# Graph layers on one core: run 5's third tile moved to TensorE, SyncE's start reordered, three smaller edits

## The chip, the cores and the metric

The kernel runs on one core of a Trainium2 chip. The metric is the device time of one execution in microseconds (us), lower is better. The engines of the core run their own instruction streams and meet at semaphores: TensorE (PE in the profile) multiplies, with its weight loads listed apart (PEld); VectorE (DVE) and ScalarE (ACT) do elementwise work; GpSimd (POOL) issues indirect gathers; SyncE (SP) issues the other transfers.

## The reference

Four layers of a graph network over 1250 nodes with 512 features and 40,000 edges, which come sorted by destination, then a residual and a layer norm:

```python
def _gine_layer(x, src, dst, edge_attr, eps, We, be, W1, b1, gamma, beta, W2, b2):
    e = edge_attr @ We + be
    m = relu(x[src] + e)
    agg = segment_sum(m, dst, num_segments=x.shape[0])
    h = ((1.0 + eps) * x + agg) @ W1 + b1
    h = (h - mean(h, axis=0)) * rsqrt(var(h, axis=0) + BN_EPS) * gamma + beta
    h = relu(h)
    return relu(h @ W2 + b2)
# four layers on x, src, dst, edge_weight1; then
x = layernorm(x + layers(x))
```

All of it is in float32.

## The kernel before

**Tiling.** The 40,000 edges are 313 tiles of 128, and a step takes 32 tiles: 10 steps a layer, the last with 25. A step works in 8 quads of tiles. For each tile, the rows x[src] + be of its 128 edges have to be in SBUF; VectorE then forms max(row, -w We) (`messages`, L1500), which is the message up to a term that is added per node, and TensorE multiplies the tile with a one-hot of the destinations inside a window of 32 nodes (`sum_quad`, L1889). Sums of 16 tiles are placed into blocks of 128 nodes (`open_block`, `add_first_pair`, `close_block`), and `product_h` (L2018) multiplies the block with W1, one step behind. After the last step come the rest of the block, the batch norm and the dense part `dense` (L2061), which also makes the next layer's table of rows.

**Two ways to a row.** Most tiles are gathered by GpSimd from the table in DRAM (`gather_quad`, L812), one indirect DMA a tile, into the slot of `rows` that an earlier quad leaves (it waits for `quad_summed`). The others, "near" tiles, hold edges whose sources lie in 256 nodes that are in SBUF as `table_parts`: VectorE makes a one-hot of the sources (`make_src_onehot`, L1327), TensorE multiplies it with the table (`gather_tiles`, four matmuls a tile, L1940), and ScalarE's relu (L991) gives the messages. The table is held in two parts, a rounded one that ScalarE makes (`hi_part`, L626) and the rest, which VectorE subtracts (`lo_part`, L633). Two partitions of each one-hot hold the edge's weight and two of each table part hold We; SyncE loads them (`load_w_rows`, L680, one for each near tile, and `load_We_rows`, L670). The source numbers of the near tiles are spread to 126 partitions in `src_bc` by `spread_src` (L711) from the DRAM array `near_srcs`.

**Runs.** In the first nine steps 8 tiles in a row are a run: 36 runs, four a step. At the start of the execution the edges of each run are reordered on the core so that its near tiles are full of near edges: the keys of the edges are turned on TensorE, moved in ten rounds (`move_lanes`, L1395), turned back, and laid down by `place_lanes` (L915) and L1438. Runs from 4 on with an even number have three near tiles, odd ones two, except the runs in `EXTRA_RUNS` (9, 13, ... 33), which have a third. In the first four runs there is one more near tile, tile 5. A layer so has 99 near tiles of 313, three tiles of the last step are loaded by SyncE row by row (`load_rows`, L694), and GpSimd gathers 211. These 7 + 4 extra tiles are collected apart: `make_extra_onehot` (L905, L909) on ScalarE makes a one-hot of 7 x 128 for each, and `sum_extra` (L1815) on TensorE sums with it; nine before the lanes are placed, two after. The results go through `finish_near` (L1459 to L1473) on VectorE to `near_srcs` and `near_ws`. A count on the core checks that each run holds as many near edges as its tiles take (128 each); where one doesn't, the flag sends all engines into a slow path that handles one tile at a time.

**Order of the work around the change.** Each engine's order is written out by hand. SyncE at the start: inputs; the ten blocks of the table as they are staged (L1407, written at L655), W1 (L664), then, when ScalarE has made `near_src` (L925), that array to DRAM (L716), its spread, the We rows, the weights of the near tiles to DRAM (L721), their rows, the extra tiles. GpSimd in each layer: 12 early gathers (`gather_early`), then `layer_begins`, which waits until the whole table is written and x is updated, a wait on `lo_ready` until all table parts are subtracted, and the other gathers in order. In the first layer also the sums of the edge weights are made: ScalarE copies them (`copy_w`), `place_w` (L1873, L1877) places them on TensorE behind quad 1, VectorE reduces them (`keep_w`, L1385) and adds them times We to u (`finish_u`). In the last step `keep_w` stands behind the messages of quad 2, ahead of those of quad 3.

## Time and profile before

| | before |
|---|---|
| median of 3 runs | 1306.46 us (1304.39 to 1312.17) |
| profiled execution, time | 1306.36 us |
| profiled execution, span | 1304.6 us |
| PE busy (share of the span) | 1196.9 us (92%) |
| DVE busy | 1030.8 us (79%) |
| POOL busy | 806.2 us (62%) |
| ACT busy | 527.2 us (40%) |
| mean granted TensorE clock | 0.949 of full |
| gathers on GpSimd | 844, 211 a layer |
| matmuls of `gather_tiles` | 1584, 4 for each of 99 tiles a layer |

The span goes from the first to the last instruction of the profiled execution. Busy shares are means over stages with different limits: the start (to some 96 us), four layers with ten steps each, and a dense part after each layer. In the rows below a line of a timeline gives the start, the duration, the engine and line, the operation with its operands, and in brackets how long the engine was idle before and what ended that. SPq is SyncE's queue issuing a DMA; the duration is the issuing alone. In the chain of waits a DMA's duration reaches to its landing.

### The profile page before, as it was taken

What the parts mean: (1) busy time and instruction counts of PE and PEld (TensorE: products, weight loads), DVE (VectorE), ACT (ScalarE), POOL (GpSimd) and SP (SyncE); (2) the same over time, 40 slices, a digit from 0 to 9 for tenths busy, and PEclk for the clock granted to TensorE, in tenths of its full rate; (3) what the DMA queues carried; (4) which work ended last, traced back from release to release, by engine and by line L of the source; (5) the groups of instructions that cost most, each with busy time, mean ns of one, the idle gap of its engine ahead of it and who ended that gap; (6) DMA issues with size and microseconds to landing.
All of it is one profiled execution on the core that took longest, in us unless ns stands there. A gap on an engine that the chain in (4) does not pass through costs nothing.

```text
span 1304.6 us, 24990 instructions
## 1 busy us (share of the span) xinstructions
PE 1196.9 (92%) x7338; PEld 750.9 (58%) x7338; DVE 1030.8 (79%) x2120; ACT 527.2 (40%) x1155; POOL 806.2 (62%) x855
## 2 busy tenths in 40 slices
PE   3838999999898999999798999999798999999797
PEld 2834666666544666566454566656455566665453
DVE  7968889888768878887767978787766978778677
ACT  1833343434274343334174334333254434334233
POOL 0047777777317777777607777777705777777720
PEclk7559999999899999999899999999798999999899
DMA  3158777777547777777737777777746777777753
GB/s 112 55 185 254 215 215 215 216 214 215 170 134 225 216 215 214 216 215 215 241 104 229 214 216 214 215 215 215 235 128 204 215 214 216 215 215 215 225 177 110
DMA packets 93131, 259.25 MB, mean 199 GB/s; under 512 B 19527, under 2 KB 22780, under 8 KB 92992
## 3 DMA queue, kind: packets, MB, share of 16 engines
q0 software_dynamic: 67520, 221.30, 58.2%
q1 hardware_dynamic: 25472, 36.29, 8.5%
q8 instruction: 63, 1.03, 0.3%
q14 instruction: 76, 0.62, 0.1%
HBM read 244.36 MB, written 12.96 MB: 197 GB/s over the span
## 4 chain that ended last, share of the span: by engine, by line
POOL 42%; PE 32%; issue 14%; DVE 8%; DMA 3%; SPq 0%; POOLq 0%; ACT 0%; DVEq 0%
POOL rows L812 42%; PE y_ps L2061 9%; PE y_ps L1940 7%; PE pair_ps L1889 6%; PE h_ps L2018 3%; DVE rows L1500 2%; DVE rows L1395 2%; PE y_ps L2072 1%; PE uT_ps L1971 1%; DMA rows<-node_table,src_fast 1%; PE uT_ps L1978 1%; PE uT_ps L1964 1%; DMA node_table<-rows 1%; PE pair_ps L2004 1%; DVE rows L1407 1%
## 5 line engine op out<-in xcount | busy, mean ns | idle before, releaser
L812 POOL DMA_INDIRECT rows<-node_table,src_fast x844 | 803.5, 952 | 444.2 <-issue 256.7
L1500 DVE SCALAR_TENSOR_TENSOR rows<-We_ps,negw_fast,rows 128x512 f32<-128x512 f32 x844 | 581.9, 743 | 155.3 <-DMA rows<-node_table,src_fast 154.6
L991 ACT ACTIVATE rows<-y_ps 128x512 f32<-128x512 f32 x396 | 234.2, 603 | 497.4 <-PE y_ps L1940 493.7
L1940 PE MATMUL y_ps<-table_parts,src_onehot 128*128 128x512 f32 x1584 | 419.1, 412 | 15.3 <-DVE table_parts L633 8.0
L1940 PEld LDWEIGHTS y_ps<-table_parts,src_onehot 128*128 128x128 f32 x1584 | 281.3, 190 | 208.3 <-issue 99.4
L1889 PE MATMUL pair_ps<-rows,onehot 128*32 128x512 f32 x2504 | 323.8, 615 | 38.8 <-DVE rows L1500 38.5
L1889 PEld LDWEIGHTS pair_ps<-rows,onehot 128*32 128x32 f32 x2504 | 62.0, 109 | 174.2 <-issue 105.5
L1327 DVE TENSOR_TENSOR src_onehot<-y_ps,src_bc 126x256 fp32r<-126x256 f32 x356 | 138.9, 412 | 3.0 <-PE y_ps L1940 3.0
L2018 PEld LDWEIGHTS h_ps<-uT,W_sb 128*128 128x128 f32 x1152 | 134.3, 192 | 7.0 <-issue 4.2
L2018 PE MATMUL h_ps<-uT,W_sb 128*128 128x128 f32 x1152 | 135.2, 276 | 0.0
L2061 PE MATMUL y_ps<-rows,hT 128*128 128x512 f32 x288 | 124.5, 593 | 0.0
L2061 PEld LDWEIGHTS y_ps<-rows,hT 128*128 128x128 f32 x288 | 54.4, 190 | 67.9 <-issue 59.8
L1091 ACT ACTIVATE hT<-hT,bn_bias,bn_scale 128x128 f32<-128x128 f32 x160 | 65.5, 480 | 6.6 <-DVE bn_bias L1546 6.6
L1004 ACT ACTIVATE hT<-h_ps,vec 128x128 f32<-128x128 f32 x144 | 41.2, 370 | 59.0 <-PE h_ps L2018 59.0
L978 ACT COPY pair_sb<-pair_ps 128x512 f32<-128x512 f32 x76 | 44.3, 583 | 42.0 <-PE pair_ps L1889 42.0
L1692 DVE TENSOR_TENSOR rows<-y_ps,b_bc 128x512 f32<-128x512 f32 x36 | 24.8, 688 | 37.4 <-PE y_ps L2061 37.4
L1315 DVE TENSOR_TENSOR onehot<-y_ps,local_all 128x512 f32<-128x512 f32 x80 | 53.5, 669 | 0.6 <-DVE w_sum L1385 0.3
L1971 PE MATMUL uT_ps<-place,pair_sb 128*128 128x96 f32 x304 | 46.0, 297 | 0.0
L1971 PEld LDWEIGHTS uT_ps<-place,pair_sb 128*128 128x128 f32 x304 | 40.5, 207 | 3.4 <-issue 3.4
L1978 PEld LDWEIGHTS uT_ps<-place,pair_sb 128*128 128x128 f32 x288 | 37.0, 201 | 6.7 <-issue 6.7
L1815 PE MATMUL h_ps<-hT 128*128 128x2 f32 x154 | 32.3, 344 | 8.3 <-ACT hT L909 8.3
L1978 PE MATMUL uT_ps<-place,pair_sb 128*128 128x64 f32 x288 | 39.4, 282 | 0.0
(248 smaller groups left out, 779.0 us busy)
## 6 DMA issues: line engine op xcount, KB each, us to landing
late_rows<-node_table SPq DMA_DIRECT2D x1536, 2.0 KB
rows<-node_table,src_fast POOLq DMA_INDIRECT x844, 3.7
node_table<-rows SPq DMA_DIRECT2D x29, 256.0 KB, 3.4
src_onehot<-near_ws SPq DMA_DIRECT2D x396, 2.0 KB
x_now<-x_pad SPq DMA_DIRECT2D x10, 512.0 KB, 7.6
W_sb<-W SPq DMA_DIRECT2D x4, 1024.0 KB, 5.3
rows<-W SPq DMA_DIRECT2D x16, 256.0 KB, 4.0
out<-rows SPq DMA_DIRECT2D x8, 256.0 KB
```

Of the source, the lines that this page charges most:

```text
L812: nc.gpsimd.indirect_dma_start(rows[:, slot, :], None, table[:, :], bass.IndirectOffsetOnAxis(src_fast[:, t:t + 1], 0)).then_inc(landed[q] ...
L991: nc.scalar.activation(rows[:, slot, :], y_ps[k % 2][:, :], ACT.Relu).then_inc(tile_ready, 1)
L1091: nc.scalar.activation(hT[:, c, at:at + P], hT[:, c, at:at + P], ACT.Relu, bias=bn_bias[:, c:c + 1], scale=bn_scale[:, c:c + 1]).then_inc( ...
L1315: return nc.vector.tensor_tensor(to, cols_ps[:, 0:WIN].unsqueeze(1).to_broadcast([P, tiles, WIN]), local_all[:, at:at + tiles].unsqueeze(2 ...
L1327: nc.vector.tensor_tensor(src_onehot[0:USED, at:at + 2, :], nodes[0:USED, :].unsqueeze(2).to_broadcast([USED, 2, P]), src_bc[0:USED, sprea ...
L1500: last = nc.vector.scalar_tensor_tensor(rows[:, slot, :], We_ps[:, :], negw_fast[:, t:t + 1], row, ALU.mult, ALU.max)
L1889: last = nc.tensor.matmul(pair_ps[h][WIN * win:WIN * (win + 1), :], onehot[:, h, tile - h * PAIR, :], rows[:, slot, :], start=t in firsts, ...
L1940: last = nc.tensor.matmul(y_ps[k % 2][:, :], src_onehot[:, 2 * (k % ONEHOTS) + b, :], table_parts[:, part, 2 * pair_of(k) + b, :], start=( ...
L1971: nc.tensor.matmul(sums_of(c, l, i)[:, 0:PLACED], pair_sb[:, 0, f], place0(i), start=False, stop=False, skip_group_check=True)
L1978: last = nc.tensor.matmul(uT_ps[:, c, HALF:P], pair_sb[:, 1, c * P:(c + 1) * P], place1(i, 0, HALF), start=False, stop=True, skip_group_ch ...
L2018: last = nc.tensor.matmul(h_ps[:, c, :], W1_sb[:, k, c * P:(c + 1) * P], uT[:, k, :], start=(k == 0), stop=(k == C - 1))
L2061: last = nc.tensor.matmul(y_ps[m % 3][:, :], hT[:, c, at:at + P], W2_sb[:, c, :], start=(c == 0), stop=(c == C - 1))
```

## The change

One more run, number 5, gets a third near tile: `EXTRA_RUNS` begins at run 5, `TWO_RUNS` becomes a single slice, `EXTRA_TILES` goes from 11 to 12 and the near tiles of a layer from 99 to 100, the gathers from 211 to 210. Nine extra one-hots stay on ScalarE; the last three (two before) are made by VectorE with a comparison, behind the subtraction of the We rows' parts and ahead of the scaling of the row numbers, and ScalarE's two are dropped. Two small arrays move into slots of `rows` that are free at that time. GpSimd no longer waits for `lo_ready` after `layer_begins`. In the first layer's last step `place_w` stands behind quad 0 instead of quad 1. SyncE writes seven blocks, then sends `near_src` to DRAM, then writes the last three blocks, sends the near weights, spreads the sources, loads the first weight rows, and only then the We rows and W1.

```diff
--- before.py
+++ after.py
@@ -103,13 +103,13 @@
     KINDS = 3
     FIRST_RUNS, LATER_RUNS = slice(0, LONG_A_STEP), slice(LONG_A_STEP, LONG_RUNS)
     THREE_RUNS = slice(LONG_A_STEP, LONG_RUNS, 2)
-    EXTRA_RUNS = slice(2 * LONG_A_STEP + 1, LONG_RUNS, LONG_A_STEP)
-    TWO_RUNS = [slice(LONG_A_STEP + 1, LONG_A_STEP + 2), slice(LONG_A_STEP + 3, LONG_RUNS, LONG_A_STEP)]
+    EXTRA_RUNS = slice(LONG_A_STEP + 1, LONG_RUNS, LONG_A_STEP)
+    TWO_RUNS = slice(LONG_A_STEP + 3, LONG_RUNS, LONG_A_STEP)
     THIRDS = (LONG_RUNS - LONG_A_STEP) // 2
     EXTRAS = list(range(LONG_RUNS)[EXTRA_RUNS])
     FIRST_EXTRA = LONG - 3
     EXTRA_TILES = len(EXTRAS) + LONG_A_STEP
-    EXTRAS_BEFORE = EXTRA_TILES - 2
+    EXTRAS_BEFORE = EXTRA_TILES - 3
     SOON_STAGED = 7
     LATER_EXTRAS, FIRST_EXTRAS = slice(0, len(EXTRAS)), slice(len(EXTRAS), EXTRA_TILES)
     EARLY_BELOW = 3 * P - MARGIN + 34
@@ -310,10 +310,10 @@
         extra_edges = hT[:, 0, GUARD + 2 * P:GUARD + 2 * P + 2 * LONG * EXTRA_TILES].rearrange("p (e j v) -> p e j v", j=LONG, v=2)
         minus_place = sb("minus_place", [P, EXTRA_TILES, LONG])
         near_first = sb("near_first", [P, LONG_A_STEP, LONG], bf16)
-        chosen_first = sb("chosen_first", [P, LONG_A_STEP, LONG])
+        chosen_first = spare(15, LONG_A_STEP * LONG, SORTED_TILES).rearrange("p (r j) -> p r j", j=LONG)
         minus_from = sb("minus_from", [P, 1])
         run_delta = sb("run_delta", [P, LONG_RUNS])
-        within = sb("within", [P, SORTED_TILES], i32)
+        within = spare(13, SORTED_TILES).bitcast(i32)
         node_in = sb("node_in", [P, 2])
 
 
@@ -597,10 +597,8 @@
                     (THREE_RUNS, slice(7, 8), last[:, rest_lanes(THREE_RUNS), 0:1]),
                     (EXTRA_RUNS, slice(3, 7), first[:, rest_lanes(EXTRA_RUNS), :]),
                     (EXTRA_RUNS, slice(7, 8), last[:, rest_lanes(EXTRA_RUNS), 0:1]),
-                    (TWO_RUNS[0], slice(2, 6), first[:, rest_lanes(TWO_RUNS[0]), :]),
-                    (TWO_RUNS[0], slice(6, 8), last[:, rest_lanes(TWO_RUNS[0]), :]),
-                    (TWO_RUNS[1], slice(2, 6), first[:, rest_lanes(TWO_RUNS[1]), :]),
-                    (TWO_RUNS[1], slice(6, 8), last[:, rest_lanes(TWO_RUNS[1]), :]),
+                    (TWO_RUNS, slice(2, 6), first[:, rest_lanes(TWO_RUNS), :]),
+                    (TWO_RUNS, slice(6, 8), last[:, rest_lanes(TWO_RUNS), :]),
                     (FIRST_RUNS, slice(2, 5), first[:, early_lanes, 0:3]),
                     (FIRST_RUNS, slice(6, 8), first[:, rest_lanes(FIRST_RUNS), 0:2])]
 
@@ -701,10 +699,11 @@
                 for c in range(C):
                     sp.dma_start(row_numbers(m)[:, c, :], src_t[ROW_PIECE * c:ROW_PIECE * (c + 1), t:t + 1].rearrange("p o -> o p"),
                                  allow_slow_non_contiguous=True).then_inc(row_numbers_loaded, 16)
-            for k in range(BLOCKS):
-                sp.wait_ge(staged, k + 1)
-                write_block(k)
-            load_W1(0)
+            def write_blocks(a, z):
+                for k in range(a, z):
+                    sp.wait_ge(staged, k + 1)
+                    write_block(k)
+
             def spread_src(g):
                 for a, z in SPREAD[g]:
                     at = SPREAD_AT[a]
@@ -712,16 +711,19 @@
                                  near_srcs[a:z, :].rearrange("(o b) p -> o (b p)", o=1).to_broadcast(
                                      [USED, (z - a) * P])).then_inc(src_spread[g], 16)
 
+            write_blocks(0, SOON_STAGED)
             sp.wait_ge(sort_act, NEAR_SRC_READY)
             sp.dma_start(near_srcs[0:P, :], near_src[:, :]).then_inc(near_src_written, 16)
+            write_blocks(SOON_STAGED, BLOCKS)
+            sp.wait_ge(sort_dve, NEAR_W_READY)
+            sp.dma_start(near_ws[0:P, :, :], near_w[:, :, :].bitcast(fp32)).then_inc(near_w_written, 16)
             sp.wait_ge(near_src_written, 16)
             spread_src(0)
-            load_We_rows(0)
-            sp.wait_ge(sort_dve, NEAR_W_READY)
-            sp.dma_start(near_ws[0:P, :, :], near_w[:, :, :].bitcast(fp32)).then_inc(near_w_written, 16)
             sp.wait_ge(near_w_written, 16)
             for k in range(EXTRA_AT):
                 load_w_rows(0, k)
+            load_We_rows(0)
+            load_W1(0)
             sp.wait_ge(extra_src_ready, 1)
             sp.dma_start(near_srcs[P:P + EXTRA_TILES, :], extra_src[0:EXTRA_TILES, :]).then_inc(near_src_written, 16)
             sp.wait_ge(extra_w_ready, 1)
@@ -845,7 +847,6 @@
                 for l in range(L):
                     gather_early(l)
                     layer_begins(l)
-                    pool.wait_ge(lo_ready, PARTS_A_LAYER * (l + 1))
                     for q in range(QUADS):
                         gather_quad(q, 0, False)
                     for i in range(1, BLOCKS):
@@ -928,9 +929,7 @@
             nc.scalar.copy(lane_values[:, 1, :], lane_ints[:, 1, :]).then_inc(sort_act, 1)
             nc.scalar.mul(near_w[:, 0, :], lanes[:, 1, 0:P].bitcast(fp32), -0.5).then_inc(sort_act, 1)
             place_lanes(src_fast, turned_src, SRC_TURNED)
-            make_extra_onehot(EXTRAS_BEFORE)
             place_lanes(negw_fast, turned_w, LAST_TURNED)
-            make_extra_onehot(EXTRAS_BEFORE + 1)
             for k in range(WRITTEN[0], BLOCKS):
                 act.wait_ge(staged, k + 1)
                 hi_part(k)
@@ -1423,6 +1422,14 @@
                                            near_w[:, 0, :], ALU.mult, ALU.subtract).then_inc(sort_dve, 1)
             dve.wait_ge(We_hi_ready, 1)
             nc.vector.tensor_tensor(We_lo[0:1, :], We_bc[0:1, :], We_hi[0:1, :], ALU.subtract).then_inc(We_parts_ready, 1)
+            then_wait(nc.vector.tensor_scalar(minus_place[:, EXTRAS_BEFORE:EXTRA_TILES, :], minus_place[:, EXTRAS_BEFORE:EXTRA_TILES, :],
+                                              -1.0, None, ALU.mult))
+            for e in range(EXTRAS_BEFORE, EXTRA_TILES):
+                dve.wait_ge(extra_summed, e - 2)
+                nc.vector.tensor_tensor(
+                    extra_onehot(e), cols[:, 0:P].unsqueeze(1).to_broadcast([P, LONG - 1, P]),
+                    minus_place[:, e, 0:LONG - 1].unsqueeze(2).to_broadcast([P, LONG - 1, P]),
+                    ALU.is_equal).then_inc(extra_onehot_ready, 1)
             dve.wait_ge(row_numbers_loaded, 16 * C * len(ROW_TILES))
             places = hT[0:len(ROW_TILES), :, ROW_GUARD:ROW_GUARD + ROW_PIECE].bitcast(i32)
             nc.vector.tensor_scalar(places, places, float(ROW_BYTES), None, ALU.mult).then_inc(row_places_ready, 1)
@@ -1900,6 +1907,8 @@
                         pe.wait_ge(pair_copied[q // 4], n + 1)
                         pe.wait_ge(onehot_ready, 2 * n + q // 4 + 1)
                     sum_quad(q, l, i)
+                    if q == 0 and l == 0 and final:
+                        place_w(i)
                     if final:
                         gather_tiles(l, QUADS * i + q)
                     elif q % 2:
@@ -1915,7 +1924,7 @@
                             product_h(n - 1, l, i - 1)
                     if q == 0 and l == 0 and i == 0:
                         sum_w(0)
-                    if q == 1 and l == 0:
+                    if q == 1 and l == 0 and not final:
                         place_w(i)
                     if q == 3 and final:
                         open_block(n, l, i, True)
```

## Rows read from the trace of the kernel before

**Rows 1.** The page: chain that ended last; costliest group (busy, mean ns | idle before).

```profile
POOL 42%; PE 32%; issue 14%; DVE 8%; DMA 3%; SPq 0%; POOLq 0%; ACT 0%; DVEq 0%
...
L812 POOL DMA_INDIRECT rows<-node_table,src_fast x844 | 803.5, 952 | 444.2 <-issue 256.7
```

**Rows 2.** Chain of waits, 60 to 135 us: start us, us, what.

```profile
74.34 5.50 DMA near_srcs<-near_src
...
80.22 5.01 DMA src_bc<-near_srcs
...
95.83 5.57 PE y_ps L1940 x16
```

**Rows 3.** Timeline of the start, in order of time: start us, us, engine line op.

```profile
71.33 0.40 ACT L925 ACTIVATE near_src<-rows,minus_from 128x128 uint8<-128x128 int32 x1
...
73.83 0.47 SPq L664 DMA_DIRECT2D W_sb<-W  x1
...
75.53 0.23 DVE L1438 COPY local_all<-pair_ps 128x64 f32<-128x64 f32 x1 [1.18 <-PE y_ps L1826]
...
76.80 0.52 DVE L1445 TENSOR_TENSOR local_all<-local_all,run_delta 128x128 f32<-128x128 f32 x4
...
80.75 3.06 PEld L1815 LDWEIGHTS h_ps<-hT 128*128 128x128 f32 x14 [2.13 <-ACT hT L909]
...
93.41 0.95 POOL L812 DMA_INDIRECT rows<-node_table,src_fast  x1 [3.64 <-DVE table_parts L633]
```

**Rows 4.** Landing of the W1 load; then DMA issues (median us to landing last).

```profile
DMA to landing us min/median/max: 5.8/5.8/5.8
...
rows<-node_table,src_fast POOLq DMA_INDIRECT x844, 3.7
...
eps_cur<-eps SPq DMA_DIRECT2D x4, 0.5 KB, 2.6
```

**Rows 5.** Timeline: a copy of 864 elements at the start; a gather before the second layer.

```profile
26.96 0.93 DVE L1309 COPY rows<-rows 128x864 f32<-128x864 f32 x1
...
395.52 1.36 POOL L812 DMA_INDIRECT rows<-node_table,src_fast  x1 [0.30 <-issue]
```

**Rows 6.** First layer, steps 0 and 1: timeline of SyncE and TensorE.

```profile
118.45 0.25 SPq L680 DMA_DIRECT2D src_onehot<-near_ws  x1
...
120.73 0.25 SPq L680 DMA_DIRECT2D src_onehot<-near_ws  x1
...
122.46 1.06 PE L1889 MATMUL pair_ps<-rows,onehot 128*32 128x512 f32 x8 [1.30 <-DVE rows L1500]
...
129.00 2.14 PE L1940 MATMUL y_ps<-table_parts,src_onehot 128*128 128x512 f32 x8
```

**Rows 7.** First layer's last step: timeline, then a window (counts, PEclk, DMA share, GB/s).

```profile
332.38 1.94 PE L1889 MATMUL pair_ps<-rows,onehot 128*32 128x512 f32 x8 [2.26 <-DVE rows L1500]
...
341.81 0.94 POOL L812 DMA_INDIRECT rows<-node_table,src_fast  x1 [0.30 <-issue]
...
342.66 0.16 DVE L1385 TENSOR_REDUCE w_sum<-h_ps 128x1 f32<-128x3 f32 x1 [5.16 <-PE h_ps L1877]
...
351.77 1.91 PE L1889 MATMUL pair_ps<-rows,onehot 128*32 128x512 f32 x12
...
330.00:342.00 12.00, 9.74 (x49) 6.15 (x46) 7.50 (x12) 1.64 (x5) 8.95 (x11) 0.57 0.80 255
```

**Rows 8.** Start of the second layer: timeline.

```profile
396.30 0.69 DVE L633 TENSOR_TENSOR table_parts<-rows,table_parts 126x512 fp32r<-126x512 f32 x1 [0.24 <-ACT table_parts L626]
...
400.08 1.09 ACT L991 ACTIVATE rows<-y_ps 128x512 f32<-128x512 f32 x2 [3.71 <-DMA node_table<-rows]
```

**Rows 9.** Third layer: timeline of TensorE, two of the products h; the waits of layer 4.

```profile
736.92 3.74 PE L2018 MATMUL h_ps<-uT,W_sb 128*128 128x128 f32 x32
...
812.89 3.74 PE L2018 MATMUL h_ps<-uT,W_sb 128*128 128x128 f32 x32
...
PE pair_ps L1889 <- DVE rows L1500: 9.4, 10, 3.1
```

## The prediction

> **What bounds the kernel now.** The profiled execution took 1306.36 us for a span of 1304.6 us. It stands 0.10 us from the median of the three runs shown (1306.46), so a difference against it is one against the median. I read the page first: the chain that ended last runs for 42% of the span through GpSimd's gathers and for 32% through TensorE [rows 1]. A gather costs 0.952 us and 0.30 us of issue behind it, 1.254 us in all, 844 times. Then the chain in order of time. It has two parts. From the start to about 360 us, where layer 1 of 4 ends, no gather is in it: it is the start (VectorE, SyncE's small transfers, VectorE again) and then TensorE. In layers 2 to 4 it follows the gathers one by one, about 250 us a layer, with the dense part between.
>
> The start has one place that waits for transfers. ScalarE has the near source numbers ready at 71.33 + 0.40 = 71.73 us [rows 3]. SyncE sends them at 74.34 only, behind the last block's write and the W1 load; they land 5.50 us later, at 79.84, and their spread to 126 partitions lands at 85.23 [rows 2]. Only then can VectorE make the first source one-hots. TensorE's first gather by matmul starts at 95.83 [rows 2].
>
> **SyncE's order.** The numbers' write now stands in front of blocks 7 to 9 and of W1. What does it take there? Ahead of it was W1, issued at 73.83 and landed after 5.8 us, at 79.6, just before the write at 79.84 [rows 3, 4]. A small transfer without such company takes 2.6 us [rows 4]. So it goes at 71.8 and lands between 74.4 (2.6) and 77.3 (5.5 again). I take 74.4, since the W1 load is what stood ahead of it. The Trainium skill (DMA: Bandwidth & Descriptors, Queues, rings and completion order) says that a DMA engine consumes one ring's descriptors in ring order; by that rule the write is free of W1 and 74.4 is right, without it the engines were merely loaded and 77.3 is.
>
> The spread takes 85.23 - 79.84 = 5.4 us again, landing at 79.8 to 82.7. Three block writes are in flight beside it, so I take 80.6: **4.6 us earlier**, with ends at 2.5 and, from VectorE's side, 5.8 us, as follows.
>
> **VectorE's new work.** The one-hots of the last three extra tiles come from ScalarE to VectorE, before the copies of rows that start at 75.53 after an idle 1.18 us and end at 76.80 + 0.52 = 77.32 [rows 3]. The trace has no comparison of 896 elements; the nearest row is a copy of 864, 0.93 us [rows 5]. I take 1.0 each, 0.9 to 1.1, and 0.2 for the sign: 3.2 us. VectorE is through at 77.32 - 1.18 + 3.2 = 79.3, before the spread at 80.6. The work is covered by that wait, with 1.3 us to spare; if the spread came earlier, 79.4 would be the floor. TensorE's three sums of 14 weight loads at 3.06 us (the slower kind, [rows 3]) end by 75.5 + 9.2 = 84.7. VectorE asks for them after its five subtractions, which ended near 92.6 and will near 88: covered.
>
> Two-input work on VectorE touches GpSimd too: a gather beside the subtractions of table parts, one of them at 396.30, took 1.36 instead of 0.95 us [rows 5, 8]. The new one-hots run beside the first early gathers: three times 0.4, 1.2 us. I count nothing, since GpSimd has slack in this layer (below). The Trainium skill (SBUF — State Buffer, Who interferes with whom) has a harder rule against this change: a VectorE instruction with two SBUF inputs keeps a GpSimd instruction that reads SBUF off the shared port for its whole length. By it the early gathers would lose up to 3.2 us; the row shows less.
>
> **The rest of SyncE's queue.** Moved back are the We rows (four DMAs) and W1. The weights' write goes at 74.0 and lands 2.6 to 5.8 us later; four weight rows and four We rows at up to 0.47 each follow, so the We rows are issued by 80.4 to 83.6 and land by 89.4 at the latest. TensorE needs them at 95.83 - 4.6 = 91.2. W1, issued by 84.1, is first read in step 1, past 130. The extra tiles' write comes at about 89.7, when W1 (by 89.9) has just landed: 0 to 0.2 us.
>
> **GpSimd's dropped wait.** In layer 1 it held the gathers back 3.64 us, to 93.41 [rows 3]. With one gather less GpSimd would be 4.9 us ahead. But it is not the bound there: its last gather is issued at 341.81 and lands 3.7 us later at 345.5 [rows 4, 7], while the last matmuls of the step stand at 351.77 [rows 7], some 6 us later. TensorE's side moves by 4.6 us, so the slack stays. The wait would also have ended with VectorE's subtractions, at 88.0. Worth 0. In later layers the last subtraction is done at 396.99, the table's write only at 400.08 [rows 8], which GpSimd waits for anyway. Worth 0.
>
> **The third tile of run 5.** Per layer it removes one gather and one VectorE message, and adds four matmuls, one source one-hot (VectorE), one relu (ScalarE) and one weight row (SyncE). Two such tiles take TensorE 2.14 us, so 1.07 each [rows 6]. Layer 1: the tile's matmuls fall in step 0, just before 122.46, where TensorE waits 1.30 us for VectorE [rows 6]. They fit. VectorE gives up a message for a shorter one-hot. Worth 0, at worst 1.1 us. Layers 2 to 4: one gather less on the path, 1.254 us each, **3.8 us**. That holds if TensorE has room. Its own pace is (812.89 - 736.92) / 3 = 25.3 us a step [rows 9]; 21 gathers take 26.3. It starts behind and catches up, and then waits for VectorE's rows, 9.4 us in layer 4 [rows 9]. The change asks 1.25 + 1.07 = 2.3 of those. Enough is left.
>
> **Weights placed behind quad 0 in the last step of layer 1.** VectorE waited 5.16 us for them [rows 7]. That goes. What is late next? TensorE itself: after 332.38 it never waits for VectorE to the end of the step (its last group ran from 351.77 without an idle, [rows 7]), and the moved matmuls are the same. The cover is TensorE's own queue. Worth 0.
>
> **Sum.** 4.6 + 3.8 = 8.4 us: 1306.36 - 8.4 = **1298.0 us**, 0.6% less. Ends: 2.5 + 3.8 - 1.1 = 5.2 gives 1301.2; 5.8 + 3.8 = 9.6 gives 1296.8; with the spread of runs, 1295.5 to 1302.
>
> **Rivals.**
> 1. The start does not move: the spread lands near 85 again since the DMA engines, not W1, are the limit. Then 3.8 remain: 1302.6. For it: three writes and the gathers run at that time. Against: the landing just behind W1. 0.09.
> 2. TensorE is the bound in layers 2 to 4: 3 x 1.07 more instead of 3.8 less, 1306.36 - 4.6 + 3.2 = 1305.0. Against: 9.4 us of waiting. 0.03.
> 3. Slower: SyncE's rows. For each near tile it sends a weight row and four late rows, one round in 120.73 - 118.45 = 2.28 us [rows 6], against 25.3 / 11 = 2.30 us a tile on TensorE. If this queue decided, each extra tile would cost 2.28 us in four layers, 9.1: 1306.36 - 4.6 + 9.1 = 1310.9. It decides where a row's issue less than some 3 us precedes its tile. The tiles at 129.00 used the row issued at 118.45 and the one after; with one tile more they use that of 120.73 first, 8.3 us ahead. 0.02.
> 4. The clock. Before the last step of layer 1 TensorE waits 2.26 us, and the next eight matmuls take 1.94 us where eight take 1.06 elsewhere [rows 6, 7]; the granted clock was 0.57 of full from 330 to 342 us, mostly the 1.2 GHz level [rows 7]. Over the 10 us from 332.4 on that costs about 10 x (1 - 1.06 / 1.94) = 4.5 us where TensorE is the path. If shifted waits spare one: 1293.5. 0.07.
> 5. The change doesn't do what it says: run 5 must hold 128 edges with sources among 252 nodes in seven tiles, else the slow path runs, far above all this. Expected are 896 x 252 / 1250 = 181. 0.01.
>
> The likeliest case has 0.78.
>
> **Range and chances.** A measurement tells 1% (13 us) from no change. Only case 4 comes to 1293.3, half of it, and a little of the likeliest: faster 0.07. Slower by over 1%: case 5 and some of 3: 0.02. The rest, 0.91, is within 1%. The range of 8 in 10 takes in the likeliest, case 1 and the edge of case 4: 1294 to 1303.
>
> **What would show it.** The numbers' write in about 2.6 us, the spread landed before 82; TensorE's first gather by matmul near 91; VectorE's one-hots about 1 us each and no wait behind them; 840 gathers; VectorE's wait of 5.16 us gone and the layer's end moved only as much as its start; layers 2 to 4 each 1.25 us shorter from the first to the last gather. I am wrong if the spread again lands 5 us after its issue behind something else, or if TensorE's waits for rows vanish in layer 4.

## The result and the profile after

The changed kernel takes 1300.35 us (median of 6 runs, 1296.56 to 1301.59), the kernel before beside it 1308.94 (6 runs, 1304.39 to 1312.17): ratio 0.9929, 95% interval [0.9911, 0.9947]. A second comparison gave 1300.31 against 1308.98 (e9, below). So it is 8.6 us less, where the forecast's sum was 8.4, and 1300.35 lies in the forecast's range of 1294 to 1303. The likeliest value, 1298.0, is 2.35 us lower, mainly since the forecast set out from 1306.36 and the median of the kernel before is 1308.94 over six runs. The profiled execution took 1299.8 us, 6.56 less than that of before.

The page of the changed kernel: chain that ended last, then the group of the gathers, which answer to [rows 1].

```profile
POOL 39%; PE 36%; issue 14%; DVE 8%; DMA 2%; ACT 0%; DVEq 0%
...
L814 POOL DMA_INDIRECT rows<-node_table,src_fast x840 | 800.3, 953 | 439.8 <-issue 256.5
```

840 gathers instead of 844; the chain is the same kind. The lines of before stand some lines lower (a gather at L814, a VectorE message at L1507, a quad's sum at L1896, a gather by matmul at L1949).

Timeline of the start of the changed kernel, SyncE, VectorE, GpSimd and TensorE, answering to [rows 2, 3]:

```profile
71.50 0.33 SPq L716 DMA_DIRECT2D near_srcs<-near_src  x1
72.00 1.53 SPq L653 DMA_DIRECT2D node_table<-rows  x3
73.58 0.45 SPq L719 DMA_DIRECT2D near_ws<-near_w  x1
74.08 0.90 SPq L710 DMA_DIRECT2D src_bc<-near_srcs  x2
...
80.01 0.45 SPq L662 DMA_DIRECT2D W_sb<-W  x1
...
74.09 3.10 DVE L1429 TENSOR_TENSOR hT<-cols,minus_place 128x896 f32<-128x896 f32 x3
...
78.48 0.52 DVE L1452 TENSOR_TENSOR local_all<-local_all,run_delta 128x128 f32<-128x128 f32 x4
80.39 1.43 DVE L1326 TENSOR_TENSOR src_onehot<-node_in,src_bc 126x256 fp32r<-126x256 f32 x4 [1.40 <-issue]
...
74.50 1.65 POOL L814 DMA_INDIRECT rows<-node_table,src_fast  x1 [71.19 <-ACT src_fast L916]
76.46 1.55 POOL L814 DMA_INDIRECT rows<-node_table,src_fast  x1 [0.30 <-issue]
...
91.08 6.73 PE L1949 MATMUL y_ps<-table_parts,src_onehot 128*128 128x512 f32 x16 [2.13 <-issue]
```

The write of the source numbers goes at 71.50. It lands in 16 parts in the trace, the last at 72.90: it takes 1.4 us, not 5.5. SyncE sends the spread, which waits for it, only at 74.08, since three block writes and the near weights stand between in its queue. The last landing of the spread in the trace is at 78.35 (85.23 in the kernel before; both traces hold 30 of its 32 landings). VectorE's first source one-hot comes 1.40 us after its last copy, at 80.39. The chain of waits shows what its queue does in that time: L1599 loads the flag of the slow path, L1763 branches on it.

```profile
79.22 0.55 DVEq L1599
79.80 0.21 DVEq L1599
80.11 0.06 DVEq L1763
```

TensorE's first gather by matmul moves from 95.83 to 91.08, **4.75 us** (4.6 forecast). VectorE's three one-hots take 3.10 us.

Where the rest went is read at TensorE's first matmuls of each layer's dense part (the part behind the last step). I call the time between two of these a layer. Before: 360.12, 661.01, 961.80, 1262.46. After: 354.88, 655.21, 955.60, 1255.90. Layer 1's end came 5.24 us earlier, but layers 2 to 4 gave only 0.56, 0.40 and 0.36 in this profile, 1.3 in sum, where 3.8 were forecast. The last step of layer 2 shows why: TensorE's timeline of the changed kernel, then a window (counts, PEclk, DMA share, GB/s).

```profile
625.64 1.94 PE L1896 MATMUL pair_ps<-rows,onehot 128*32 128x512 f32 x8 [3.70 <-DVE rows L1507]
...
635.68 1.94 PE L1896 MATMUL pair_ps<-rows,onehot 128*32 128x512 f32 x8
637.55 4.94 PE L2027 MATMUL h_ps<-uT,W_sb 128*128 128x128 f32 x32
642.41 1.06 PE L1896 MATMUL pair_ps<-rows,onehot 128*32 128x512 f32 x8
```

```profile
619.00:640.00 21.00, 16.29 (x72) 9.31 (x73) 15.17 (x24) 2.41 (x4) 15.94 (x17) 0.51 0.78 246
```

Eight matmuls of 512 columns take 1.94 us here and 1.06 behind it: TensorE was granted the level of 1.2 GHz for some 20 us, after waits for VectorE's rows. From quad 0's sum, at 625.64, to the dense part took 29.57 us; in the kernel before 28.18, with a low stretch of some 10 us:

```profile
629.00:649.00 20.00, 16.18 (x100) 10.84 (x100) 13.92 (x22) 2.44 (x5) 15.12 (x17) 0.74 0.82 261
```

So layer 2 reached its last step 1.9 us sooner and gave 1.4 back there; in the mean of layers 2 to 4 it is 1.5 and 1.1. Whether it does so each time is what experiment e9 had to settle.

In layer 1's last step the order of the placed weights is changed as the diff says. The changed kernel, TensorE, then VectorE, answering to [rows 7]:

```profile
328.18 1.07 PE L1896 MATMUL pair_ps<-rows,onehot 128*32 128x512 f32 x8 [2.25 <-DVE rows L1507]
329.17 0.53 PE L1880 MATMUL h_ps<-pair_w,place 128*128 128x3 f32 x2
...
333.22 0.14 DVE L1384 TENSOR_REDUCE w_sum<-h_ps 128x1 f32<-128x3 f32 x1
...
350.13 0.42 DVE L1595 COPY uT<-y_ps 128x256 f32<-128x256 f32 x1 [3.63 <-PE y_ps L1998]
```

VectorE's 5.16 us of waiting are gone, and it waits 3.63 us for TensorE later: TensorE was the cover, as forecast. GpSimd issued its last gather of the layer at 338.37 (341.81 before), 3.4 us earlier, not the 4.9 of the forecast.

### The profile page after: what moved, and what is told of

The parts are those of the page before. It is cut to its first block, busy times and chain, and to the rows that moved or that the text cites. A ratio compares the mean times of both kernels' runs of the same rounds, so it can differ in the third digit from the quotient of the medians.

```text
span 1298.0 us, 25044 instructions
## 1 busy us (share of the span) xinstructions
PE 1205.2 (93%) x7367; PEld 759.7 (59%) x7367; DVE 1032.9 (80%) x2122; ACT 523.0 (40%) x1139; POOL 803.0 (62%) x851
## 4 chain that ended last, share of the span: by engine, by line
POOL 39%; PE 36%; issue 14%; DVE 8%; DMA 2%; ACT 0%; DVEq 0%
POOL rows L814 39%; PE y_ps L2070 10%; PE y_ps L1949 7%; PE pair_ps L1896 7%; PE h_ps L2027 3%; DVE rows L1507 2%; DVE rows L1394 2%; PE uT_ps L1980 1%; PE y_ps L2081 1%; PE uT_ps L1987 1%; PE uT_ps L1973 1%; DMA rows<-node_table,src_fast 1%; PE uT_ps L1962 1%; DMA node_table<-rows 1%; PE pair_ps L2013 1%
## 5 line engine op out<-in xcount | busy, mean ns | idle before, releaser
L814 POOL DMA_INDIRECT rows<-node_table,src_fast x840 | 800.3, 953 | 439.8 <-issue 256.5
L1507 DVE SCALAR_TENSOR_TENSOR rows<-We_ps,negw_fast,rows 128x512 f32<-128x512 f32 x840 | 579.2, 742 | 156.8 <-DMA rows<-node_table,src_fast 156.1
L1949 PE MATMUL y_ps<-table_parts,src_onehot 128*128 128x512 f32 x1600 | 420.9, 409 | 13.9 <-DVE table_parts L631 8.0
L1949 PEld LDWEIGHTS y_ps<-table_parts,src_onehot 128*128 128x128 f32 x1600 | 282.5, 189 | 207.8 <-issue 94.8
L1896 PE MATMUL pair_ps<-rows,onehot 128*32 128x512 f32 x2504 | 322.2, 616 | 33.9 <-DVE rows L1507 33.4
L1896 PEld LDWEIGHTS pair_ps<-rows,onehot 128*32 128x32 f32 x2504 | 62.2, 109 | 167.2 <-issue 103.1
L2027 PEld LDWEIGHTS h_ps<-uT,W_sb 128*128 128x128 f32 x1152 | 137.2, 196 | 8.5 <-issue 5.8
L2027 PE MATMUL h_ps<-uT,W_sb 128*128 128x128 f32 x1152 | 138.1, 279 | 0.0
L1822 PE MATMUL h_ps<-hT 128*128 128x2 f32 x168 | 36.5, 353 | 4.8 <-ACT hT L910 4.8
```

Of the source, the lines that this page charges most:

```text
L814: nc.gpsimd.indirect_dma_start(rows[:, slot, :], None, table[:, :], bass.IndirectOffsetOnAxis(src_fast[:, t:t + 1], 0)).then_inc(landed[q] ...
L1507: last = nc.vector.scalar_tensor_tensor(rows[:, slot, :], We_ps[:, :], negw_fast[:, t:t + 1], row, ALU.mult, ALU.max)
L1896: last = nc.tensor.matmul(pair_ps[h][WIN * win:WIN * (win + 1), :], onehot[:, h, tile - h * PAIR, :], rows[:, slot, :], start=t in firsts, ...
L1949: last = nc.tensor.matmul(y_ps[k % 2][:, :], src_onehot[:, 2 * (k % ONEHOTS) + b, :], table_parts[:, part, 2 * pair_of(k) + b, :], start=( ...
L2027: last = nc.tensor.matmul(h_ps[:, c, :], W1_sb[:, k, c * P:(c + 1) * P], uT[:, k, :], start=(k == 0), stop=(k == C - 1))
```

## Experiments

All times below are medians, and the ratios are to the kernel before, run beside them on the same chip. Experiments e1 to e4 shared one comparison, e5 to e8 another, e9 to e12 a third; only the third has the changed kernel in it. Where a dense part is dated, it is TensorE's first matmul there in the profiled execution.

**e1, SyncE's old order** (the other three parts kept).

```
-            write_blocks(0, SOON_STAGED)
+            write_blocks(0, BLOCKS)
+            load_W1(0)
             sp.wait_ge(sort_act, NEAR_SRC_READY)
             sp.dma_start(near_srcs[0:P, :], near_src[:, :]).then_inc(near_src_written, 16)
...
```

> The changed kernel with SyncE's order at the start as it was (W1 and all ten blocks ahead of the source numbers). Theory A (the start's gain is SyncE's order alone): the numbers' write again takes about 5.5 us, the spread lands near 85, TensorE's first gather by matmul starts at 95 to 96 instead of 91.08 us, the dense part of layer 1 begins about 4.7 us later than 354.88, the whole near 1304.5 us against 1299.8 for the changed kernel's profiled execution. Rival B (the start was won by taking one-hots off ScalarE or by the dropped wait): first gather by matmul stays near 91 and the time near 1300.

1302.2 us (4 runs), ratio 0.9944 [0.9926, 0.9963]. SyncE's and VectorE's timeline of e1:

```profile
74.07 0.55 SPq L717 DMA_DIRECT2D near_srcs<-near_src  x1
80.00 0.77 SPq L710 DMA_DIRECT2D src_bc<-near_srcs  x2
...
85.55 1.43 DVE L1325 TENSOR_TENSOR src_onehot<-node_in,src_bc 126x256 fp32r<-126x256 f32 x4 [6.56 <-DMA src_bc<-near_srcs]
```

The write takes 5.9 us again and the first gather by matmul starts at 96.29, as theory A had it. The whole gain of the start is SyncE's order. Layer 1's dense part began at 362.76, 7.9 us later than in the changed kernel and not 4.7: its last step had a longer stretch at the low clock (table below).

**e2, without the third tile of run 5.**

```
-    EXTRA_RUNS = slice(LONG_A_STEP + 1, LONG_RUNS, LONG_A_STEP)
-    TWO_RUNS = slice(LONG_A_STEP + 3, LONG_RUNS, LONG_A_STEP)
+    EXTRA_RUNS = slice(2 * LONG_A_STEP + 1, LONG_RUNS, LONG_A_STEP)
+    TWO_RUNS = [slice(LONG_A_STEP + 1, LONG_A_STEP + 2), slice(LONG_A_STEP + 3, LONG_RUNS, LONG_A_STEP)]
...
```

> The changed kernel without run 5's third tile (99 near tiles and 211 gathers a layer; VectorE still makes three extra one-hots). Theory A (in layers 2 to 4 the time from one dense part to the next is set by the low clock in the last step, which swallowed most of the tile's gain): these distances, 300.33, 300.39 and 300.30 us with the tile, become 300.7 to 300.9 without it, so the whole is 1.3 us slower. Rival B (the tile is worth its gather, 1.25 us a layer, and something else in the change cost 0.8 a layer): they become 301.6, the whole 3.8 us slower.

1302.93 us (6 runs), ratio 0.9961 [0.994, 0.9982]; 844 gathers. Its dense parts start at 358.45, 659.37, 959.75 and 1261.66: layers of 300.92, 300.38 and 301.91 us. From a dense part to quad 0 of the next last step it takes 272.03, 271.49, 271.77 us, against 270.77 in the mean with the tile. From the 13th gather of a layer (the first behind the early ones) to its last it takes 247.6 us here in each of layers 2 to 4, against 246.3 to 246.6 in all profiles with the tile: one gather, 1.25 us. (In the kernel before it is 248.2: in that profile each gather took 3 ns more than in e2.) The layers fit neither theory by themselves, since their last steps differ by more than the theories do.

**e3, a busy TensorE ahead of the last steps.** 16 products without a use stand in the queue ahead of quad 0 of each layer's last step, so that its wait is filled.

```
+                if final:
+                    idle_products(y_ps[0][:, :], KEEP)
                 for q in range(QUADS):
```

> The changed kernel with 16 products that nobody reads on TensorE ahead of quad 0 of the last step of each layer, about 4 us, where it waits 2.3 us in layer 1 and 3.6 to 4.2 us in layers 2 to 4 for the messages. Theory A (the idle wait lowers the clock, and the low clock then sets the tail): the last step's eight matmuls take 1.06 instead of 1.94 us, product h 3.8 instead of 4.9, and each layer from 2 on is about 1.3 us shorter, until the last gather (12.2 us ahead of the dense part in the kernel before) sets the end; layer 1 gains 2 to 4 us: 1292 to 1295 in all. Rival B (the landing of the last gathers sets the end anyway): the clock is up but the distances between the dense parts stay at 300.3 us and the time at 1298 to 1300; if the products only delay quad 0, 1300 to 1302.

1295.69 us (4 runs), ratio 0.9908 [0.9888, 0.9929]. In layer 1's last step the clock was 1.00 throughout. In layers 2 to 4 quad 0's wait shrank to 1 us and its sum ran at full clock, but the low level came at a later wait; TensorE's timeline of e3, layer 4:

```profile
1222.43 1.06 PE L1897 MATMUL pair_ps<-rows,onehot 128*32 128x512 f32 x8 [1.01 <-DVE rows L1508]
...
1230.45 1.94 PE L1897 MATMUL pair_ps<-rows,onehot 128*32 128x512 f32 x8 [2.29 <-DVE rows L1508]
1232.31 5.79 PE L2030 MATMUL h_ps<-uT,W_sb 128*128 128x128 f32 x32
```

From quad 0 to the dense part it still took 28.59, 29.44 and 28.39 us. Layer 1's dense part came at 353.07, 1.8 us earlier, and the time lies between the two theories.

**e4, two one-hots of extra tiles on VectorE instead of three.**

```
-    EXTRAS_BEFORE = EXTRA_TILES - 3
+    EXTRAS_BEFORE = EXTRA_TILES - 2
```

> The changed kernel with one of VectorE's three extra one-hots made by ScalarE, which idles 8.03 us before the lanes are placed. Theory A (VectorE, not the spread of the source numbers, now sets the start: its last copy ends at 79.00, and the 1.40 us before its first source one-hot at 80.39 are the branch): everything from there on is 1.0 us earlier, first gather by matmul at 90.0, whole near 1298.8. Rival B (the spread's landing sets 80.39): the first source one-hot stays at 80.39 and the time at 1299.8.

1296.75 us (4 runs), ratio 0.9912 [0.9893, 0.9931]. The chain of waits of e4, then VectorE's timeline:

```profile
74.25 1.40 SPq L710
...
75.70 4.24 DMA src_bc<-near_srcs
```

```profile
80.05 1.45 DVE L1326 TENSOR_TENSOR src_onehot<-node_in,src_bc 126x256 fp32r<-126x256 f32 x4 [1.83 <-DMA src_bc<-near_srcs]
```

The first source one-hot comes at 80.05 instead of 80.39, the first gather by matmul at 90.73. One us less of VectorE's work gained only 0.35, since here the spread sets the start, landing at 79.93. In the changed kernel it had landed by 78.4: there VectorE was the later of the two, by about 2 us. The spread is 1.6 us later in e4 since SyncE took 1.40 us to issue its first half (0.44 in the changed kernel). The same is seen in e11 and e12, the other two kernels with two one-hots on VectorE (1.3 and 1.2 us); the cause stays open. The profiled execution's gain over that of the changed kernel, 4.4 us, came almost whole in the last steps of layers 2 to 4, in code that is the same: there the low stretches were shorter, and layer 1's dense part moved by only 0.1 us.

**e5, W1 ahead of the numbers' write**, the rest of SyncE's order as changed.

```
             sp.wait_ge(sort_act, NEAR_SRC_READY)
+            load_W1(0)
             sp.dma_start(near_srcs[0:P, :], near_src[:, :]).then_inc(near_src_written, 16)
...
             load_We_rows(0)
-            load_W1(0)
```

> The W1 load stands ahead of the near source numbers' write again, the rest of SyncE's order is that of the changed kernel. Theory A (the write took 5.5 us before because the W1 load was in front of it): W1 is issued near 71.5 us, the write some 0.5 us later and it lands only with W1, 5 to 6 us after its issue, near 77.5; the spread lands near 83 and TensorE's first gather by matmul starts near 94 instead of 91.1; time about 3 us above the changed kernel's, near 1303. Theory B (the write took long since the DMA engines were loaded at that time by the gathers and block writes, not because of W1): it lands 2.6 us after its issue as in the changed kernel, the first gather by matmul at 91.1 to 91.6, the time the same.

1302.41 us (10 runs), ratio 0.9949 [0.9933, 0.9965]. The chain of waits of e5:

```profile
71.60 0.39 SPq L662
...
72.03 6.41 DMA near_srcs<-near_src
...
78.84 5.48 DMA src_bc<-near_srcs
```

Theory A: the same write, 0.5 us later, takes 6.4 us behind the W1 load and 1.4 us ahead of it, and the first gather by matmul goes to 95.11. Theory B, that gathers and block writes were the cause, falls. The trace holds 16 landings for W1, at 77.12 to 78.28, and 16 for the write, at 77.31 to 78.44: it lands part by part just behind the load. Three block writes issued right behind the write in the changed kernel did it no harm.

**e6, weights placed behind quad 1 again in the last step.**

```
-                    if q == 0 and l == 0 and final:
-                        place_w(i)
...
-                    if q == 1 and l == 0 and not final:
+                    if q == 1 and l == 0:
```

> In layer 1's last step the weights are placed behind quad 1 again. Prediction's step (worth 0, TensorE's own queue is the cover): VectorE's wait of about 5 us for the placed weights comes back, and the time from quad 0 of that step to layer 1's dense part is within 0.5 us of the changed kernel's, apart from the clock. Rival (VectorE's wait delayed something): layer 1's dense part starts 2 us or more later than at 354.9.

1294.85 us (4 runs), ratio 0.9906 [0.9879, 0.9933]: if anything faster than with the step. TensorE's, then VectorE's timeline of e6:

```profile
327.96 1.07 PE L1896 MATMUL pair_ps<-rows,onehot 128*32 128x512 f32 x8 [2.26 <-DVE rows L1507]
...
333.24 0.34 PE L1880 MATMUL h_ps<-pair_w,place 128*128 128x3 f32 x2
...
333.98 0.16 DVE L1384 TENSOR_REDUCE w_sum<-h_ps 128x1 f32<-128x3 f32 x1 [0.89 <-PE h_ps L1884]
```

VectorE's wait is back, but with 0.89 us, not 5.16. Neither theory had that: the wait of before was long since TensorE ran that step at the low level. The wait is 0.89 us with no low stretch (e6), 2.51 with 3.4 us of one (e10) and 5.16 with 10.2 us (before). Layer 1's dense part started at 351.43, 3.45 us earlier than in the changed kernel, behind a quad 0 that differs by 0.22 us. The windows of that step, changed kernel, then e6:

```profile
328.00:338.00 10.00, 9.82 (x58) 6.67 (x58) 9.96 (x18) 1.30 (x3) 7.56 (x9) 0.66 0.81 256
```

```profile
328.00:338.00 10.00, 10.00 (x86) 7.34 (x87) 9.07 (x16) 1.83 (x3) 7.56 (x9) 1.00 0.90 293
```

**e7, GpSimd's wait for the table's split put back.**

```
                     layer_begins(l)
+                    pool.wait_ge(lo_ready, PARTS_A_LAYER * (l + 1))
```

> GpSimd waits for the split of the table again ahead of a layer's first gather. Prediction's step (worth 0): GpSimd starts its main gathers of layer 1 at the end of VectorE's subtractions, within 0.5 us of 88, and layer 1's dense part starts within 0.5 us of 354.9; in layers 2 to 4 nothing moves. Rival (without the wait GpSimd starts layers earlier): the first gathers of layer 1 come 1 us or more later than without the wait, and the time rises by as much.

1298.12 us (9 runs, 1294.23 to 1304.08), ratio 0.9935 [0.9917, 0.9952]. GpSimd's timeline of e7:

```profile
90.00 0.95 POOL L814 DMA_INDIRECT rows<-node_table,src_fast  x1 [0.30 <-issue]
91.25 0.95 POOL L814 DMA_INDIRECT rows<-node_table,src_fast  x1 [0.30 <-issue]
```

The gather at 90.00 is the last of the 12 early ones, that at 91.25 the first behind the wait. It is not held: with the start 4.7 us earlier the subtractions end at 87.57, before GpSimd gets to this wait at 90.95. The wait is worth 0, as forecast, but the gathers do not start at the subtractions' end near 88, as expected; the early ones end later than that. Layer 1's dense part began at 353.93, 0.95 us earlier than in the changed kernel.

**e8, weights placed right behind the quad's sum in every step** (quad 1, in the last step quad 0), ahead of the gathers by matmul.

```
-                    if q == 0 and l == 0 and final:
+                    if q == (0 if final else 1) and l == 0:
                         place_w(i)
...
-                    if q == 1 and l == 0 and not final:
-                        place_w(i)
```

> The weights of a block are placed on TensorE right behind the sum of quad 1 in every step of layer 1 (quad 0 in the last), ahead of the gathers by matmul that follow that sum. Theory A (the 2.26 us that TensorE waits for VectorE before layer 1's last step, and the stretch at the 1.2 GHz level behind it, come from VectorE's wait of 3.9 us for the placed weights in the step before): VectorE's wait falls under 1 us, TensorE's wait of 2.26 us shrinks under 1 us, the granted clock stays high in that step, and layer 1's dense part starts 3 to 6 us earlier than 354.9; layers 2 to 4 unchanged; time 1294 to 1298. Theory B (TensorE's wait comes from VectorE's own amount of work): VectorE's wait goes, but TensorE's stays about 2 us and the dense part moves by less than 1 us.

1295.95 us (4 runs), ratio 0.991 [0.9884, 0.9935]. Theory A holds for layer 1: clock 1.00 in its last step, dense part at 350.02, 4.86 us earlier. TensorE is no longer what this layer waits for. The chain of waits of e8, from the last but one gather of layer 1:

```profile
335.58 0.95 POOL rows L814
336.83 3.59 DMA rows<-node_table,src_fast
...
350.02 10.38 PE y_ps L2068 x24
```

The gathers now set the end of layer 1: once TensorE gains 4.9 us, nothing is left of the slack that the forecast put at some 6 us.

**e9, the changed kernel again**, unaltered, with more rounds.

> The changed kernel unaltered, run again with more rounds beside the kernel before, so that its time and its layers do not rest on one profiled execution. Theory A (the four parts are worth what the prediction's sum says, 8.4 us, and the first profile of the changed kernel only caught long stretches at the 1.2 GHz level): its layers 2 to 4 take about 299.1 us each in the profile, not 300.3, and the median stands 8 to 10 us below the kernel before. Theory B (the tail of the last step eats 1.1 us of each layer's gain every time): layers of 300.3 again and a median 6 to 7 us below.

1300.31 us (6 runs, 1295.97 to 1301.43), ratio 0.9928 [0.9909, 0.9948], 8.67 us below the kernel before (1308.98, 11 runs). Its layers took 300.44, 299.59 and 299.15 us, between the two theories (the median is in theory A's range): the first of the three had again a low stretch of 20 us and 29.59 us from quad 0 to the dense part, the others 28.93 and 28.12.

**e10, weights behind quad 1 again, a second time** (the edit of e6).

> The kernel with the weights placed behind quad 1 again in layer 1's last step, a second time, beside the changed kernel. Theory A (the place of these matmuls decides nothing; the profile of the first such run had the full clock in that step by chance): over 5 rounds its median is within 1.5 us of the changed kernel's of the same call. Theory B (behind quad 0 they bring on the stretch at the 1.2 GHz level in layer 1's last step, which then costs 3 us): the granted clock in that step is 1.00 again, the time from quad 0 to the dense part 23.5 us against 25.0, and the median is 2 to 4 us below the changed kernel's.

1296.75 us (5 runs), ratio 0.991 [0.9891, 0.9928]: 3.6 us below e9, as theory B had it, but the clock fell here too, for about 3 us. Below the two are taken apart.

**e11, combination**: e3's 16 products, e4's two one-hots, e8's place.

> Weights placed right behind the sum of quad 1 (quad 0 in the last step), 16 products without a use ahead of quad 0 in every layer's last step, and two instead of three one-hots of extra tiles made by VectorE. Theory A (the gains add as far as the chain lets them; GpSimd's gathers bound layer 1 now): dense part of layer 1 starts at 349.5 to 350.5, layers 2 to 4 take 298.4 to 299.2 each, time 1291 to 1295. Theory B (the clock takes back what one place gains): layers of 299.5 to 300.5, time as the changed kernel's within 2 us.

**1294.43 us** (5 runs, 1291.61 to 1294.8), ratio 0.9887 [0.9869, 0.9905]. That beats the kernel before by 14.6 us and the changed one, in the same comparison, by 5.9. Dense parts at 350.70, 650.90, 949.49, 1248.77; the layers took 300.20, 298.59 and 299.28 us. Time and layer 1 came nearly as theory A had them (350.70 against 349.5 to 350.5), the layers only in part: one of three lies within its 298.4 to 299.2. Several single edits stand within 2.3 us of the combination (e3, e4, e6, e8, e10) and their intervals overlap with its own, so that it beats each of them is not shown.

**e12, combination with 8 more products ahead of quad 2** of the last step.

```
                 for q in range(QUADS):
+                    if q == 2 and final:
+                        idle_products(y_ps[0][:, :], KEEP_2)
```

> As the combination, with 8 more products without a use ahead of quad 2 in each last step. Theory A (the low stretch, which came at the later wait of 2.3 us once quad 0's was filled, goes when that wait is filled too): the granted clock is 1.00 through the last 28 us of layers 2 to 4, the time from quad 0 to the dense part is 25 to 27 us instead of 28 to 29.5, layers 2 to 4 take 297 to 298, time 1287 to 1291. Theory B (TensorE waits for rows, and a higher clock there only makes it wait longer): the clock is 1.00, but the layers take 298.5 or more and the time is that of the combination within 1 us.

1293.85 us (5 runs, 1291.56 to 1296.29), ratio 0.9893 [0.9875, 0.991], as e11. The window of layer 4's last step in e12, then TensorE's timeline near its end:

```profile
1218.00:1248.00 30.00, 27.25 (x192) 18.40 (x190) 23.15 (x51) 5.31 (x15) 14.80 (x16) 1.00 0.63 206
```

```profile
1238.66 1.06 PE L1898 MATMUL pair_ps<-rows,onehot 128*32 128x512 f32 x6 [0.63 <-DVE rows L1509]
1240.26 1.70 PE L1898 MATMUL pair_ps<-rows,onehot 128*32 128x512 f32 x6 [0.54 <-DVE rows L1509]
```

Theory B: the full clock in all four last steps, yet 28.03, 28.23 and 27.71 us from quad 0 to the dense part, and layers of 299.53, 298.89 and 298.28. TensorE now waits for the last rows; the gathers are the floor of layers 2 to 4. From a layer's last gather to the dense part it takes 11.9 to 12.2 us here, and 11.8 to 14.2 in the other profiles.

## Why the prediction held, step by step

**The start: 4.6 forecast, 4.75 measured.** The mechanism is right: e1 and e5 show that the W1 load alone made the write slow (1.4 us without it in front, 5.9 and 6.4 behind it). The Trainium skill's rule of ring order (DMA: Bandwidth & Descriptors, Queues, rings and completion order) agrees with that. That the two sums are so close is in part luck, since sizes inside the step were off and nearly cancelled:

- The write took 1.4 us, not 2.6, but SyncE came to the spread only at 74.08, near the forecast's 74.4.
- The spread then took 4.3 us, not 5.4 and more, and had landed by 78.4, not 80.6.
- VectorE was through with its copies at 79.0 (79.3 forecast), but ready only at 80.39, since the forecast left out the 1.40 us of loading the flag and branching. "Covered, with 1.3 us to spare" was wrong: VectorE was the later, by about 2 us.

So the start is now set by VectorE and not, as the forecast had it, by the spread; by the forecast's own floor for that case the gain would have been 5.8 us.

**SyncE's later rows.** W1 was issued at 80.01, well inside the 84.1 allowed, and the extra tiles' write went at 89.59 (89.7 forecast). The rival of SyncE's rows (1310.9) fell with the time.

**VectorE's one-hots.** 3.10 us against 3.2. Two early gathers beside them took 1.65 and 1.55 us; at the same place in the kernel before 1.11 and 0.95, so 1.1 us lost, forecast 1.2. The Trainium skill's harder rule (SBUF — State Buffer, Who interferes with whom), read as a block for as long as VectorE works on the three, would have cost up to 3.1 us here; the rows show a third of that. Each of the two gathers lost less (0.54 and 0.60 us) than one of these instructions lasts (1.09 and 1.08), so a block by a single instruction is not ruled out. Two more early gathers were slowed, which the forecast did not count: one beside the source one-hots took 1.16 us and one beside the subtractions 1.41. So GpSimd's gathers behind the early ones began at 91.50, and GpSimd gained 3.4 us in layer 1 where the forecast had 4.9; its slack shrank, but it was enough.

**The dropped wait: 0.** Right (e7).

**The third tile: 3.8.** In the first profile it was 1.3, and this was the term that looked mis-sized. Over all profiles it was not. The 27 layers of the nine kernels that have the tile, and no added products, run from a dense part to quad 0 of the next last step in 270.68 us in the mean (270.32 to 271.55), the six of before and e2 in 272.02 (271.49 to 272.71): **1.34 us a layer**, for the 1.254 of one gather and its issue. The part behind took 28.51 with it (27.62 to 29.91) and 28.91 without (28.18 to 30.14), whole layers 299.19 and 300.93. So 1.3 us are taken away before the last step and nothing is given back on average; the changed kernel's first profile drew three of the longest last steps, 29.53 to 29.62. By the ratios, the tile is worth 0.0032 to 0.0033 of 1309 us, 4.2 to 4.3 (e2 against the changed kernel, whose intervals overlap). The rival that TensorE becomes the bound (1305.0) fell: in layer 4 TensorE still waits 9.4 us for VectorE's rows, as much as before. The forecast's 2.3 us that the tile would take out of these waits are not seen.

In layer 1 the tile cost nothing that can be seen: first gather by matmul to quad 0 of the last step 237.10 us with it, 239.53 without (e2), 236.55 before. But over e1, e3 to e7, e9 and e10, which have the tile, it scatters from 236.1 to 238.3, so a cost of up to 1.1 us, the forecast's worst case, is not ruled out.

**The placed weights: 0.** At an equal clock this is right. What decides the last step of layer 1 is how long TensorE is at the low level; whether the place of these matmuls has a part in that stays open (below). From quad 0's sum to the dense part, beside the time at the low level in that step (summed from the granted clock of windows of 1 us):

```
kernel    placed behind   at 1.2 GHz, us   quad 0 to dense part, us
e6        quad 1           0               23.47
e10       quad 1           3.4             25.09
after     quad 0           6.8             26.70
e7        quad 0           6.8             26.67
e4        quad 0           6.8             26.70
before    quad 1          10.2             27.74
e9        quad 0          10.2             27.76
e2        quad 0          10.2             27.85
e5        quad 0          10.2             27.80
e1        quad 0          13.7             29.83
```

At the same low time the two places differ by 0.1 us (before against e9, e2 and e5), and each us at the low level costs 0.4 to 0.5 us. e3 and e11, with added products and quad 0, had no low stretch and took 23.60, again 0.1 from e6. Two kernels without a low stretch took longer: e8 with 25.17 us, where the gathers set the end, and e12 with 25.51, with 8 more products in the step. This is rival 4 as a mechanism: that a low stretch is spared was priced at 4.5 us and is worth up to 4.3 (27.74 - 23.47). In the changed kernel's profile it came to 1.0. With it the 5.24 us of layer 1's end add up: 4.75 from the start and 1.04 from here, less 0.55 that lay between the first gather by matmul and that quad 0 (237.10 us against 236.55).

**What stays open.** e6 and e10 together have a median of 1295.5 us over 9 runs, the changed kernel 1300.3 over 12. In the profiles of the table the low stretches behind quad 1 were 0, 3.4 and 10.2 us long, behind quad 0 never under 6.8. It may be that the thin matmuls of the placed weights (128x3) just behind the waits of 1.26 and 2.25 us keep the clock low longer; in e1, e2, e5 and e9, though, the clock fell before they ran, and e4 and e7, with the change's place, had 1296.75 and 1298.12. The changed kernel, e4 and e7 together have 1298.15 over 25 runs, still 2.6 us above e6 and e10. Three profiles on one side do not settle it: this part of the change may be worth 0, or may cost some 3 to 5 us. For the same reason the medians of single undone parts do not add up: e1 stands 1.9 us above the changed kernel and e5 2.1, where the positions in the trace show 5.2 and 4.0 at the start. Medians of kernels that differ from the changed one only by parts forecast at 0 go from 1294.85 to 1298.12, against 1300.3 for itself. So it is luck too that the whole came out within 0.2 us of the sum; what is shown is the gain at the start and the gather less in each layer.

In layers 2 to 4 a low stretch costs less, since the gathers cover it: with 6.8 us of it, 27.77 to 28.51 us from quad 0 on, with none 27.7 to 28.2 (e12), and stretches of 17 us and over gave 28.97 to 29.62. When one comes matters too: a total of 10.2 us, part of it in the last 10 us before the dense part, gave 29.91 (e10, layer 3).

## What to carry to other kernels

Put the small transfer that others wait for ahead of the large load in its queue; whether the load is what delays it shows in one look, when it lands just behind the load. Read a transfer's time from its landing, not from when the queue sends what waits for it: the queue may be busy with other things until then. Count the loading of a flag and the branch on it (1.40 us here) on an engine's path when you judge what is "covered" by a wait of about 1 us. And do not read a change of a few us from one profile: take each layer at fixed marks, over all kernels that share its code, and read the granted clock of the last step beside it.

## What the runs showed of the hardware

A write of 16 KB (128x128 uint8) behind a load of 1 MB in the same queue took 5.5 to 6.4 us (before, e1, e5), with its landings just behind those of the load; ahead of it, and ahead of three writes of 256 KB, 1.4. Loading a flag and branching on it kept VectorE from its next instruction for 1.40 us. Beside VectorE's comparisons of 128x896 elements an indirect gather's 0.95 to 1.11 us became 1.55 to 1.65. TensorE's low level began after waits for rows of 2 to 5 us in most last steps, but not in all with the same waits: e6 waited 2.26 us ahead of quad 0 at 1.00, e10 the same 2.26 us and fell. Its stretches in a last step lasted from 3 to over 20 us in the same code. Products without a use moved the low stretch from quad 0's wait to the next long one (e3), and filled both (e12); with the gathers as the floor that was worth nothing clear of noise beyond e11.
